# Attention scores: the high-times-low products made on 64 rows each, the two halves of the keys on the two halves of the array

## What is computed

```
q = (_ln(x, lnq_s, lnq_b) @ Wq + bq).reshape(Bq, Sq, H, HD).transpose(0, 2, 1, 3)
k = (_ln(x, lnk_s, lnk_b) @ Wk + bk).reshape(Bq, Sq, H, HD).transpose(0, 2, 1, 3)
v = (_ln(x, lnv_s, lnv_b) @ Wv + bv).reshape(Bq, Sq, H, HD).transpose(0, 2, 1, 3)
scores = jnp.einsum('bhqd,bhkd->bhqk', q, k) / SMAX
mask = jnp.triu(jnp.full((Sq, Sq), -999.0, dtype=scores.dtype), k=Sq - 1)
p = jax.nn.softmax(scores + mask, axis=-1)
att = jnp.einsum('bhqk,bhkd->bhqd', p, v).transpose(0, 2, 1, 3).reshape(Bq, Sq, AHD)
h = att @ Wo + bo + x
```

## Time and profile before

| | us |
|---|---|
| median of 3 runs | 2441.58 (2441.37 to 2449.67) |
| the profiled execution, its own time | 2440.7 |
| its span, first to last instruction | 2438.9 |
| first score matmul to last, attention | 290 to 1973 |
| one iteration of 32 steps in the steady state | 105.3 |

### The profile page before, as it was taken

The page is one execution under the profiler, slowest core; times in us unless marked ns, Lnnn a source line. Parts: engine busy times, 40 slices in busy tenths (PEclk is TensorE's granted clock), DMA queues, the critical chain, the costliest instruction groups (busy, mean ns, idle before and its releaser), DMA issues.

```text
span 2438.9 us, 46253 instructions
## 1 busy us (share of the span) xinstructions
PE 2382.4 (98%) x14472; PEld 2066.2 (85%) x14472; DVE 1865.4 (76%) x3615; ACT 1693.0 (69%) x2932; POOL 1512.4 (62%) x1536
## 2 busy tenths in 40 slices
PE   8999899999999999999999999999999999999999
PEld 7888778888888888888888888888888879988888
DVE  7887677878878788887878878787887875466675
ACT  4555577878878787877878778787887865443443
POOL 1333378777777777767787777777777754542220
PEclk9999999999999999999999999999999999999999
DMA  4744531222212132221213312122221345431332
GB/s 179 267 160 162 198 113 44 87 80 84 95 44 86 53 97 71 72 95 44 86 61 95 97 41 95 44 86 80 84 95 43 108 156 169 139 116 64 126 130 82
DMA packets 131969, 245.66 MB, mean 101 GB/s; under 512 B 7290, under 2 KB 90132, under 8 KB 120052
## 3 DMA queue, kind: packets, MB, share of 16 engines
q1 hardware_dynamic: 131828, 244.15, 30.8%
HBM read 140.12 MB, written 53.67 MB: 79 GB/s over the span
## 4 chain that ended last, share of the span: by engine, by line
PE 81%; DVE 8%; issue 5%; POOL 2%; ACT 2%; DMA 1%; SPq 0%; DVEq 0%; ACTq 0%; POOLq 0%
PE a_ov L1693 19%; PE a_sc L1657 18%; PE a_tr L1669 18%; PE a_pj L1612 7%; PE a_pj L1621 4%; PE g_acc L963 3%; PE g_hid L921 3%; PE f_acc L963 2%; PE f_hid L921 2%; PE m_proj L2096 1%; POOL m_zin L1948 1%; PE m_hid L2162 1%; DVE f_hp L735 1%; DVE f_gated L730 1%; DVE a_pT L1580 1%
## 5 line engine op out<-in xcount | busy, mean ns | idle before, releaser
L1569 DVE TENSOR_REDUCE a_nmax<-a_sc 128x1 f32<-128x1024 f32 x512 | 626.8, 1224 | 261.6 <-PE a_sc L1657 253.4
L1496 POOL TENSOR_SCALAR a_pr<-a_pr,a_rden 128x1024 f32<-128x1024 f32 x512 | 575.8, 1126 | 260.8 <-DVE a_rden L1574 191.4
L1412 ACT ACTIVATE a_pT<-a_tr 128x512 fp32r<-128x512 f32 x1024 | 560.1, 596 | 208.9 <-PE a_tr L1669 205.0
L1580 DVE TENSOR_TENSOR a_pT<-a_tr,a_pT 128x512 fp32r<-128x512 f32 x1024 | 650.0, 677 | 17.2 <-ACT a_pT L1412 17.2
L1693 PE MATMUL a_ov<-a_pT,a_v_s 128*128 128x512 f32 x2048 | 598.6, 414 | 3.1 <-DVE a_half L1560 2.0
L1418 ACT ACTIVATE a_pr<-a_sc,a_nmax 128x1024 f32<-128x1024 f32 x512 | 573.7, 1120 | 32.8 <-DVE a_nmax L1569 29.3
L1657 PE MATMUL a_sc<-a_k_s,a_q_s 128*128 128x512 f32 x2048 | 554.5, 392 | 3.3 <-DMA a_k_s<-a_k_s 3.3
L1669 PEld LDWEIGHTS a_tr<-f_ident,a_pr 128*128 128x128 f32 x4096 | 474.4, 140 | 92.3 <-DVE a_pT L1580 19.1
L1669 PE MATMUL a_tr<-f_ident,a_pr 128*128 128x128 f32 x4096 | 538.6, 274 | 9.3 <-DVE a_pT L1580 9.1
L1657 PEld LDWEIGHTS a_sc<-a_k_s,a_q_s 128*128 128x128 f32 x2048 | 380.2, 188 | 83.5 <-DMA a_k_s<-a_k_s 3.5
L1693 PEld LDWEIGHTS a_ov<-a_pT,a_v_s 128*128 128x128 f32 x2048 | 346.3, 189 | 53.9 <-issue 4.9
(11 more groups left out here) (252 smaller groups left out, 3220.8 us busy)
## 6 DMA issues: line engine op xcount, KB each, us to landing
a_z_s<-zT SPq DMA_DIRECT2D x32, 1024.0 KB, 7.7
a_k_s<-a_k_s SPq DMA_DIRECT2D x62, 512.0 KB, 5.7
a_wqk_s<-w_split SPq DMA_DIRECT2D x64, 256.0 KB, 3.1
a_v_s<-a_v_b SPq DMA_DIRECT2D x16, 1024.0 KB, 4.5
att<-a_ao SPq DMA_DIRECT2D x32, 512.0 KB, 2.9
m_in<-att SPq DMA_DIRECT2D x16, 1024.0 KB, 6.1
f_gB<-f_gate_rows SPq DMA_DIRECT2D x12, 1024.0 KB, 5.0
g_gB<-g_gate_rows SPq DMA_DIRECT2D x12, 1024.0 KB, 4.7
```

Source lines behind the costliest of these rows:

```text
L1412: act.activation(pT[:, (u // 4) % 2, 0, 4 * part:4 * part + 4, (u % 4) * P:(u % 4 + 1) * P], tr[:, part].rearrange("p (t q) -> p t q", t=4 ...
L1496: pool.tensor_scalar(pr[:, k % NP], pr[:, k % NP], rden[:, k % NP:k % NP + 1], 1.0, ALU.mult, ALU.mult).then_inc(s["normed"], 1)
L1569: dve.tensor_reduce(nmax[:, k % NP:k % NP + 1], sc[:, k % 2], AX.X, ALU.max, negate=True).then_inc(s["negmax"], 1)
L1580: dve.tensor_tensor(to[:, 1], tr[:, part].rearrange("p (t q) -> p t q", t=4), to[:, 0].bitcast(F32), ALU.subtract).then_inc(s["tr_lo"], 1)
```

## The change

Low x low is dropped, and high x low is made on 64 rows. The lows of the keys are no longer doubled: those of the first 512 keys lie in rows 0 to 63 and those of the second 512 keys in rows 64 to 127, for both heads (`k_lo`). For a matmul on 64 rows the high queries have to stand in the same rows as the low keys. For one half of the keys they do in `q_s`; for the other half a second copy is needed, `q_x`, with the highs of each head in the other head's rows. Both new arrays lie in the room of `k_s`, so the program's names for them read `a_k_s`. In a step, PE makes two matmuls of 128 rows with the high keys and then two of 64 rows, one on the upper and one on the lower half of the rows, into two banks.

```
-    k_s = m.sb("k_s", [P, 2, 2, 2, S], F32R, room=rooms.first)
+    k_s = m.sb("k_s", [P, 2, 4, S], F32R, room=rooms.first)
+    k_lo = k_s[:, :, 2].rearrange("p s (h k) -> p s h k", h=2)
+    q_x = k_s[:, :, 3]
...
         else:
-            hi = [k_s[r0, pair_slot, 0, 0, cols], k_s[r1, pair_slot, 1, 0, cols]]
-            lo = [k_s[r0, pair_slot, 0, 1, cols], k_s[r1, pair_slot, 1, 1, cols]]
+            hi = [k_s[r0, pair_slot, 0, cols], k_s[r1, pair_slot, 1, cols]]
+
+            lo = [k_lo[rows_of_head(part), pair_slot, head] for head in range(2)]
         return (staged[r0, slot], staged[r1, slot]), hi, lo
+
+    def across(part, pair_slot):
+
+        cols = slice(part * BT, part * BT + BT)
+        return q_x[rows_of_head(1), pair_slot, cols], q_x[rows_of_head(0), pair_slot, cols]
...
             pool.tensor_scalar(hi[0], x0, 1.0, 1.0, ALU.mult, ALU.mult).then_inc(s["head0_hi"], 1)
+            if kind == "Q":
+                for x, to in zip((x0, x1), across(part, pair_slot)):
+                    pool.tensor_scalar(to, x, 1.0, 1.0, ALU.mult, ALU.mult)
             pool.tensor_scalar(hi[1], x1, 1.0, 1.0, ALU.mult, ALU.mult).then_inc(s["head1_hi"], 1)
...
                     for kb in range(S // BT):
-                        for a in range(2):
-                            o = pe.matmul(sc[:, k % 2, kb * BT:(kb + 1) * BT],
-                                          q_s[:, slot, head, tile * P:(tile + 1) * P],
-                                          k_s[:, slot, head, a, kb * BT:(kb + 1) * BT],
-                                          start=(a == 0), stop=(a == 1))
+                        pe.matmul(sc[:, k % 2, kb * BT:(kb + 1) * BT],
+                                  q_s[:, slot, head, tile * P:(tile + 1) * P],
+                                  k_s[:, slot, head, kb * BT:(kb + 1) * BT], start=True, stop=False)
+                    for kb in range(S // BT):
+
+                        r = rows_of_head(kb)
+                        q_hi = q_s[r, slot, head] if kb == head else q_x[r, slot]
+                        o = pe.matmul(sc[:, k % 2, kb * BT:(kb + 1) * BT], q_hi[:, tile * P:(tile + 1) * P],
+                                      k_lo[r, slot, head], start=False, stop=True)
                     o.then_inc(s["sc"], 1)
```

More of the change, by code:

```diff
@@ L1257, in double_first @@
             for head, (a, b) in enumerate(((0, HD), (HD, 0))):
-                sp.dma_start(k_s[b:b + HD, 0, head, :, cols].bitcast(F32), k_s[a:a + HD, 0, head, :, cols].bitcast(F32))\
+                sp.dma_start(k_s[b:b + HD, 0, head, cols].bitcast(F32), k_s[a:a + HD, 0, head, cols].bitcast(F32))\
                     .then_inc(s["k_dup"], 16)
@@ L1487, in on_gpsimd @@
             else:
-                (x0, _), hi, _ = parts_of(kind, part, n % 2, 0)
+                (x0, x1), hi, _ = parts_of(kind, part, n % 2, 0)
                 pool.wait_ge(s["staged"], n + 1)
+                if kind == "Q":
+                    for x, to in zip((x0, x1), across(part, 0)):
+                        pool.tensor_scalar(to, x, 1.0, 1.0, ALU.mult, ALU.mult)
                 pool.tensor_scalar(hi[0], x0, 1.0, 1.0, ALU.mult, ALU.mult).then_inc(s["head0_hi"], 1)
```

## The result

| | us |
|---|---|
| before, median of 4 runs | 2444.22 (2441.37 to 2449.67) |
| after, median of 4 runs | 2498.77 (2497.96 to 2500.67) |
| ratio | 1.0226, 95% interval 1.0209 to 1.0243: about +55 |
| one iteration in the steady state, before and after | 105.3 and 109.0 |

A forecast was written before the change was run, and what follows sets the result against it. PE was taken to set the pace, with POOL one wait behind. Sixteen first stretches (29.3 us) and 14 second ones (18.1), less 12.0 gained outside them, gave +35 us, 2477 us; range 2436 to 2545.

The forecast's parts named there:

- What bounds the kernel: Attention loop: PE sets the pace, working 98% of the span; POOL is one wait behind it.
- two stretches: POOL runs nearly without waiting, keys of step 1 to tile 10 and step 17 to tile 26; PE's gain there worth nothing.
- POOL's part: Two more copies per query piece, 0.70 us each; PE 1.83 us later at tile 10, 1.29 at tile 26.
- g: Time a step gains on PE from the paired 64-row products: taken as 0.15 us, bounds -0.48 to 0.227.
- PE's part: Score products of each step: two 64-row products side by side save at most 0.227 us, 116 us gross over 512 steps.
- Outside the stretches: The eight other steps of an iteration: PE gains 0.5 us after tile 10 and 2g, 0.30, after tile 26.
- rival 3: Score products: changing the array's shape is dear, every step pays from g below about -0.11; 2590 to 2688 us; chance 0.13.
- the first rival: Score products: the 64-row halves run one after the other, g 0 to -0.10; 2489 to 2498 us; chance 0.12.
- The halves in turn: Score products: the two 64-row matmuls don't run side by side, +47 to +56 us; chance 0.12.
- Copies hidden: POOL's lateness is harmless and PE's gain shows: 2393 us, or 2339 were POOL no bound; chance 0.13.
- The dear shape: PE's shape changes, two per step, cost 0.29 to 0.48 us a step net: 2590 to 2688 us; chance 0.13.
- Cancelling: Spare time half a microsecond larger per stretch and copies at 0.62 us, both sides cancel: 2430 to 2453 us; chance 0.12.

The follow-up runs named there:

- e2: Kernel before plus POOL's two extra copies of each query piece, without the 64-row products: 2486.29 us, ratio 1.0184.
- e4: Kernel before without the fourth score product of a step, plus POOL's two extra copies of each query piece: 2473.63 us, ratio 1.012.
- e6: Changed kernel without POOL's two extra copies, both 64-row products on the same half of the array's rows: 2592.39 us, ratio 1.0605.
- e8: Changed kernel with query highs crossed by DMA and, in twelve steps of an iteration, two tiles' short products made together: 2487.31 us, ratio 1.0168.
- e3: Kernel before with the fourth score product of a step left out (second half of the keys without lows): 2397.8 us, ratio 0.9813.

## Why the prediction was right, and where not

**What bounds the kernel: right.** POOL is one wait behind PE, and the ends of its two stretches are where e2 and e4 show PE waiting. The earlier trace rows carried that, though POOL is busy only 62% of the span.

**POOL's part: right, to a tenth.** For the first stretch the forecast was +1.83, for the second +1.29; the copies alone gave 37.11 - 35.43 = 1.68 and 39.08 - 38.00 = 1.08, and with a g of nothing +47 was forecast, where e2 gave +46. What is over lies in small things: in the kernel after (POOL's timeline) two copies from start to start take (1088.82 - 1087.46) / 2 = 0.68, not 0.70, and the hand-over to PE is 0.13, not 0.2, since the normalising that starts at 1203.03 ends at 1204.15 and tile 6 is transposed at 1204.28.

```profile
1087.46 1.29 POOL L1478 TENSOR_SCALAR a_k_s<-a_staged 64x512 fp32r<-64x512 f32 x2
1088.82 0.62 POOL L1479 TENSOR_SCALAR a_q_s<-a_staged 64x512 fp32r<-64x512 f32 x1
...
1203.03 1.12 POOL L1510 TENSOR_SCALAR a_pr<-a_pr,a_rden 128x1024 f32<-128x1024 f32 x1 [0.36 <-DVE a_rden L1588]
```

**PE's part: the step that failed.** "I take g = 0.15, nearer to the top, since the rows show weights always loading under the matmul ahead, even between products of different length." Length isn't shape. By the timeline of the kernel after, g = (0.91 - 0.97) + (0.79 - 0.85) = -0.12. Two products in the time of one did give 0.227 (e6), but a way in and out costs 0.35: the later start ahead of the pair 0.10, the load of the pair 0.10, the later start behind it 0.10, and 0.05 to 0.06 at the first transposes. The bound that counted two tails without loads (-0.10) was near; the value taken wasn't, and neither was the lower end, -0.48.

The Trainium skill ("TensorEngine Tiling (Array Packing)", Key Properties) says that changing the tiling mode drains TensorE, and the traces agree, with 0.32 in place of 0.227 ahead of each change; the drain itself has no row. It also says ("TensorE: Matmul & The Clock Gate", Part 3) that matmuls on different row groups start a few ns apart; the two rows of 1085.69 agree, to the 10 ns in which rows are given.

**Outside the stretches: wrong by the same term.** There the forecast had -(0.5 + 2g) = -0.80 per iteration. It is (14.63 - 14.18) + (18.08 - 17.72) = +0.81. And "the sum below depends on it little" held only down to -0.11: it had rival 3 begin there, and the loss is -0.12 in a plain step and (36.46 - 35.43) / 12 = 0.09 and (39.20 - 38.00) / 12 = 0.10 a step over the two stretches, right at that threshold, so that PE and POOL come out almost equal in the second (39.20 and 39.08). The sum again with measured terms: 1.67 + 1.20 + 0.81 = 3.68 per iteration; 15 x 3.68 = 55, as measured.

**How much of it was luck.** The forecast's own mechanism gives +33 with the gain in it (e4) and +47 without any (e2). The missing 20 us come from a term with the wrong sign. It didn't turn the sign of the whole, since POOL's term, the larger one, was right, and in the stretches it covered most of PE's loss; and the time fell inside the range because that had been drawn well past the forecast's own 2462 to 2492, for rivals. By its number alone the first rival (2489 to 2498) came nearest, and its mechanism is refuted.

**The rivals.** The halves in turn: refuted by the common start and by e6. Copies hidden: refuted by e2. The dear shape: right in kind, PE does pay everywhere outside the first stretch, but at 0.12 a step instead of 0.29 or more. So the outcome is half the forecast's mechanism and half that of rival 3 at its threshold. Cancelling: refuted by the time.

**The signs announced.** Iterations longer by 2.4: it was 3.7. POOL busier by 85 to 90: 78, since the time from start to start (0.70) had been put for the busy time (0.61). PE waiting for POOL 3 to 8 us per iteration: 7.1 us in the fourteen from 400 to 1960 us, 0.5 in each, a miss. The waits were counted as if PE were early by its gain at each step; with a loss in its place, PE comes late by itself and waits only for tiles 6 and 10. Score start to first transposes 0.68 to 0.91: 0.97, and this one sign already told the failed step.

**The low keys' DMA.** The wait of 3.3 us ahead of the first scores is 1.8 after; nothing else of it shows.

## What to carry to other kernels

Whether row packing pays is decided by the change of array shape, not by the matmul: here a way in and out costs 0.35 us, one and a half full products of 512 columns, so a pair that saves one product (0.23) loses; by these numbers two pairs behind one change win 0.10 on PE. Steps 4 and 5 of e8 bring that in (3.06 + 3.66 = 6.72 for 2.71 + 4.10 = 6.81 before); the whole iteration doesn't, since most of the steps behind a double pair don't follow PE, four of them held by ACT. Before a product is saved, look at what is late next: of a whole product less per step (e3) less than two fifths arrived. And two costs on one loop don't add when they lie on different chains that run side by side: measure each alone, and both, stretch by stretch.

## What was unexpected of the hardware

- Ahead of a change of shape, the next matmul starts 0.32 us after the one before, not 0.227; behind it the first is 0.10 longer (0.49 to 0.50 for 0.39), full or on 64 rows alike. Four such changes a step instead of two, with the short products apart, cost 305 us over 512 steps, some 200 of it the changes.
- A second pair of the same shape behind the first costs only 0.24 and has its loads hidden (0.39).
- Two short products on different row halves start and end together, though they come as two instructions.
- POOL's copy to the other half of the rows (L1478) costs no more than the one that stays (L1475), by the groups of the kernel after from 400 to 1960 us (busy us, mean ns, idle before):

```profile
L1478 POOL TENSOR_SCALAR a_k_s<-a_staged 64x512 fp32r<-64x512 f32 x114 | 70.0, 614 | 8.4
...
L1475 POOL TENSOR_SCALAR a_q_s<-a_staged 64x512 fp32r<-64x512 f32 x57 | 34.9, 612 | 15.5 <-POOL a_pr L1510 15.2 <-ACT a_staged L1381 0.3
```
